# Scattering into the output itself, with a bound on the row index, and adding the head blocks four at a time

## The reference

```python
xn = _layernorm(x)
x = x + attn(xn, Wq, bq, Wk, bk, Wv, bv) + ffn(xn, g1, Wq, Wdkv, Wuk, Wuv, Wo, g2, gate_w, w1, w2)
# attn: per token, the 16 heads of that token attend to each other (16 x 16 scores of 16 values)
# ffn:  h = xn + mla(rmsnorm(xn, g1))        causal attention along the sequence, 16 heads of 16
#       h + moe(rmsnorm(h, g2))              8 experts 256 -> 512 (silu) -> 256, the two best of each token,
#                                            weighted by a softmax over their two logits
```

## Time and profile before

| | us |
|---|---|
| median of 3 runs | 2903.67 (2902.66 to 2905.32) |
| profiled execution, its own time | 2890.86 |
| its span in the trace | 2889.0 |
| PE, DVE, POOL, ACT busy | 2543.6, 2236.6, 2113.7, 1606.6 |

### The profile page before, as it was taken

How to read it: one execution, slowest core, us unless ns; L and a number is a source line. 1 busy time by engine, 2 the same in 40 slices (tenths; PEclk the granted TensorE clock), 3 DMA queues, 4 the chain that set the end, 5 groups by cost and what they waited for, 6 DMA issues and landing times. The chain is left out here.

```text
span 2889.0 us, 58374 instructions
## 1 busy us (share of the span) xinstructions
PE 2543.6 (88%) x21356; PEld 1302.9 (45%) x21356; DVE 2236.6 (77%) x3720; ACT 1606.6 (56%) x2421; POOL 2113.7 (73%) x1196
## 2 busy tenths in 40 slices
PE   7999878999999999999999999996673988988892
PEld 4544432333333333333333333224563877777782
DVE  5557858899889988998899989902563899889970
ACT  2322225677777777777777777684442544444441
POOL 4543339698889888988898889884675777778772
PEclk9999999999999999999999999997775999999996
DMA  5785552133233323332333232105865565566555
GB/s 179 228 251 196 170 183 60 49 80 93 53 85 87 93 53 85 87 93 53 84 87 93 54 85 77 44 19 161 263 213 172 116 126 124 122 127 131 126 91 145
DMA packets 235945, 334.91 MB, mean 116 GB/s; under 512 B 30024, under 2 KB 175272, under 8 KB 234920
## 3 DMA queue, kind: packets, MB, share of 16 engines
q1 hardware_dynamic: 208072, 287.54, 34.4%
q0 software_dynamic: 27360, 39.73, 8.0%
q10 hardware_dynamic: 256, 4.19, 0.4%
HBM read 246.96 MB, written 154.04 MB: 139 GB/s over the span
## 5 line engine op out<-in xcount | busy, mean ns | idle before, releaser
L1047 DVE TENSOR_REDUCE p_piece_max<-p_ring 128x1 f32<-128x512 f32 (+3 forms) x2160 | 1293.2, 654 | 136.8 <-PE p_ring L157 66.8
L1105 ACT ACTIVATE p_probs<-p_st 128x1024 f32<-128x1024 f32 (+3 forms) x1280 | 1078.8, 897 | 413.9 <-PE p_st L1168 215.7
L1168 PE MATMUL p_st<-unit_q,unit_k 64*128 64x512 bf16 (+3 forms) x3520 | 432.7, 348 | 39.5 <-ACT p_probs L1105 23.2
L1186 PE MATMUL p_pv<-p_probs,unit_vg 128*32 128x512 f32 (+3 forms) x3520 | 412.1, 543 | 0.0
L1855 POOL DMA_INDIRECT acc<-p_y,p_rows x142 | 223.3, 1573 | 142.7 <-issue 56.1
L170 PE MATMUL p_ring<-unit_k,unit_q 64*128 64x512 bf16 (+3 forms) x1600 | 271.4, 352 | 27.9 <-DVE p_piece_max L1047 25.4
L964 POOL TENSOR_TENSOR p_terms<-p_head_in 128x4096 f32<-128x4096 f32 x32 | 282.9, 8839 | 8.9 <-DMA p_head_in<-head_qkv 4.6
L985 POOL TENSOR_TENSOR p_terms<-p_head_p,p_head_in 128x4096 f32<-128x4096 f32 x32 | 283.3, 8853 | 3.6 <-ACT p_head_p L1112 3.6
L2020 PE MATMUL p_y_ps<-p_w,p_hid 128*128 128x256 f32 x1136 | 276.8, 400 | 0.0
L969 POOL TENSOR_TENSOR p_terms<-p_terms 128x2048 f32<-128x2048 f32 (+2 forms) x96 | 252.7, 2632 | 17.4 <-POOL p_terms L969 11.4
L991 POOL TENSOR_TENSOR p_terms<-p_terms 128x2048 f32<-128x2048 f32 (+2 forms) x96 | 252.6, 2631 | 17.1 <-POOL p_terms L991 11.4
(11 more groups left out here) (192 smaller groups left out, 3477.5 us busy)
## 6 DMA issues: line engine op xcount, KB each, us to landing
p_w<-ffn_w SPq DMA_DIRECT2D x142, 512.0 KB
qk_parts<-p_parts SPq DMA_DIRECT2D x64, 384.0 KB, 3.6
head_qkv<-p_heads SPq DMA_DIRECT2D x16, 1536.0 KB, 6.8
p_rows<-rows_by_expert SPq DMA_DIRECT2D x71, 258.0 KB, 3.5
unit_q<-qk_parts SPq DMA_DIRECT2D x132, 128.0 KB, 3.2
unit_k<-qk_parts SPq DMA_DIRECT2D x132, 128.0 KB, 3.6
v_padded<-p_vx SPq DMA_DIRECT2D x16, 1024.0 KB, 8.0
p_head_in<-head_qkv SPq DMA_DIRECT2D x32, 384.0 KB, 4.2
```

What stands on the lines that cost most here:

```text
L1047: nc.vector.tensor_reduce(piece_max[:, n % 2, h:h + heads, i, pc], ring_ps[g % RING][:, 0:heads * width].rearrange("p (h k) -> p h k", h=h ...
L1105: nc.scalar.activation(probs[:, 2 * turn_of(s, i) + u, :, 0:width], st_ps[u][:, :, 0:width], ACT.Exp).then_inc(probs_done, 1)
L1168: last = nc.tensor.matmul(st_ps[u][:, half, 0:width], k6[s][rows, PAIR * second + u, kt * P:(kt + 1) * P], q6[s][rows, PAIR * second + u, ...
L1186: last = nc.tensor.matmul(pv_ps[hh * VW:(hh + 1) * VW, skip:CT], vg[s][:, kt, hh * VW:(hh + 1) * VW], probs[:, 2 * turn_of(s, i) + hh % PA ...
```

## The change

`acc` is gone as a tensor of its own. Phase 3's `store_res` writes to the output, and phase 4's scatters and additions go to the output's rows. So the two phases need the output's address, and are called from `phase5_combine`; `phase3_route` and `phase4_experts` only keep their arguments until then. The order of the work on the engines is the same. The zeros behind row T are not written any more, and a token number above T - 1 in a scatter is left out by a bound on the index. The copy of `acc` to the output is left out, with its block. The head blocks' additions are made once in 8 tiles (n = 14, 22, ... 70), with four blocks (512 KB) in one DMA, 8 of them.

```diff
-def phase3_route(nc, apart, x_v, xn_v, o_v, w, sorted_rows, res_v, pos_v, gates_v, table):
+def phase3_route(*args):
+    SHARED["route"] = args
+def phase4_experts(*args):
+    SHARED["experts"] = args
+def route(nc, apart, x_v, xn_v, o_v, w, sorted_rows, res_v, pos_v, gates_v, table, out_v):
...
-    acc = SHARED["acc"] = nc.dram_tensor("acc", [T + ROW_TILE, D], F32, kind="Internal").ap()
-    acc_v = acc[0:T, :].rearrange("(b c t p) d -> b c p t d", b=B, c=NC, p=P)
...
-                sp.dma_start(acc_v[b, c], res[:, c % 2, :, :]).then_inc(res_stored[c % 2], 16)
+                sp.dma_start(out_v[b, c], res[:, c % 2, :, :]).then_inc(res_stored[c % 2], 16)
...
-            sp.dma_start(acc[T:, :].rearrange("(r p) d -> p r d", p=P), blank[:, :, 0:D]).then_inc(tail_stored, 16)
...
-            wait_apart(sp, tail_stored, 16 * 2 * E, apart)
+            wait_apart(sp, tail_stored, 16 * (2 * E - 1), apart)
...
-def phase4_experts(nc, apart, head_qkv, w, sorted_rows, expert_rows, attn_rows, table):
+def experts(nc, apart, head_qkv, w, sorted_rows, expert_rows, attn_rows, table, out_v):
...
-    sorted_rows, acc, table_i = SHARED["sorted"], SHARED["acc"], SHARED["table"]
+    sorted_rows, table_i = SHARED["sorted"], SHARED["table"]
+    acc = out_v.rearrange("b c p t d -> (b c t p) d")
...
-    ADDED = {STARTS[2 * k + 4] + 2: k for k in range(NB // 2)}
+    ADDED = {STARTS[4 * k + 6] + 2: k for k in range(NB // 4)}
...
-                if pairs[0]:
-                    pool.wait_ge(pair_added, 16 * pairs[0])
+                if fours[0]:
+                    pool.wait_ge(four_added, 16 * fours[0])
                 for t in range(RT):
                     nc.gpsimd.indirect_dma_start(
                         acc, bass.IndirectOffsetOnAxis(rows[:, n % RB, t, D + 1:].bitcast(U32), 0), y[:, n % RB, t, :], None,
-                        compute_op=ALU.add).then_inc(y_added, 16)
+                        bounds_check=T - 1, oob_is_err=False, compute_op=ALU.add).then_inc(y_added, 16)
-            def add_pair(k, tiles):
+            def add_four(k, tiles):
                 for u in range(2):
-                    pool.wait_ge(oh_stored[u], 16 * (k + 1))
+                    pool.wait_ge(oh_stored[u], 16 * 2 * (k + 1))
                 pool.wait_ge(y_added, 16 * RT * tiles)
-                n = block_of(2 * k, 1)
-                rows_of_pair = lambda a: a.rearrange("(r s) d -> r (s d)", s=8)
-                nc.gpsimd.dma_start(rows_of_pair(acc[n * P:(n + 2) * P, :]),
-                                    rows_of_pair(attn_rows[n:n + 2, :, :].rearrange("a p d -> (a p) d")),
-                                    accum_op=ALU.add, max_dma_last_dim=4 * 8 * D).then_inc(pair_added, 16)
-                pairs[0] += 1
+                n = block_of(4 * k, 0)
+                halves = lambda a: a.rearrange("(c h r s) d -> c h r (s d)", c=2, h=2, s=8)[:, 1, :, :]
+                nc.gpsimd.dma_start(halves(acc[n * P:(n + 8) * P, :]),
+                                    halves(attn_rows[n:n + 8, :, :].rearrange("a p d -> (a p) d")),
+                                    accum_op=ALU.add, max_dma_last_dim=4 * 8 * D).then_inc(four_added, 16)
+                fours[0] += 1
...
 def phase5_combine(nc, apart, res_v, attn_v, pos_v, gates_v, expert_rows, out_v):
-    acc = SHARED["acc"][0:T, :].rearrange("(b c t p) d -> b c t p d", b=B, c=NC, p=P)
-    with SHARED["stack"], ExitStack() as ctx:
-        stored = [ctx.enter_context(nc.semaphore(f"p5_stored{i}")) for i in range(2)]
-        block = ctx.enter_context(nc.Block())
-        def store(eng, i):
-            for b in range(B):
-                for c in range(i * NC // 2, (i + 1) * NC // 2):
-                    eng.dma_start(out_v[b, c].rearrange("p t d -> t p d"), acc[b, c]).then_inc(stored[i], 16)
-            wait_apart(eng, stored[i], 16 * B * NC // 2, apart)
...
+    route(*SHARED["route"], out_v)
+    experts(*SHARED["experts"], out_v)
+    SHARED["stack"].close()
```

More of the change, by code:

```diff
@@ L1734, in phase4_experts @@
     SHIFTED = {STARTS[m + 1]: m for m in range(NB)}
-    assert all(ADDED[n] * 2 + 1 in [m for at, m in STORED.items() if at < n] for n in ADDED)
-    assert max(ADDED) < N_TILE and max(STORED) < N_TILE and len(ADDED) == NB // 2 and len(LOADED) == NB - QB
+    assert all(ADDED[n] * 4 + 3 in [m for at, m in STORED.items() if at < n] for n in ADDED)
+    assert max(ADDED) < N_TILE and max(STORED) < N_TILE and len(ADDED) == NB // 4 and len(LOADED) == NB - QB
     with ExitStack() as ctx:
@@ L1788, in phase4_experts @@
         oh_stored = [sem(f"p4_oh_stored{i}") for i in range(2)]
-        pair_added = sem("p4_pair_added")
+        four_added = sem("p4_four_added")
         block = ctx.enter_context(nc.Block())
@@ L1844, in weigh @@
                     ins.then_inc(pv_done, 1)
-            pairs = [0]
+            fours = [0]
             def add_tile(n):
@@ L1880, in _ @@
                     weigh(m, slice(heads.start, heads.stop - 2), False)
-                add_pair(ADDED[n], n)
+                add_four(ADDED[n], n)
                 if weighed:
@@ L1885, in _ @@
             pool.wait_ge(y_added, 16 * RT * N_TILE)
-            pool.wait_ge(pair_added, 16 * NB // 2)
+            pool.wait_ge(four_added, 16 * NB // 4)
         @block.vector
```

## The result

The change makes the kernel slower: 2989.22 us median (2986.72 to 2990.06, 4 runs) against 2903.91 (4 runs), ratio 1.0292, interval 1.0274 to 1.031. Forecast were 2859 us, and 2885 at most.

A forecast was written before the change was run, and what follows sets the result against it. POOL with its pair additions was taken to bound the expert stage, DVE close behind. Terms of -32.9, -12.9, -0.8 and +2.0 summed to -44.6 us, taking 2903.67 to 2859 us; range 2837 to 2885.

The forecast's parts named there:

- Part 2: Four-block additions in place of pairs in the expert stage: 2.4 us more landing, 66.15 us per 8-tile cycle against 70.7.
- the check: The bound on the row index in each of the 142 scatters, forecast to cost 0.15 us a scatter.
- part 4: Stage edges: -0.8 us where the pair at n = 66 goes, +2.0 us behind the stage.
- Closing copy: End of the kernel: dropping the copy to the output saves 32.9 us, or 29.7 if the block's closing stays.
- Part 3: Index bound on the scatters: 0.15 us each, +2.4 us per 8-tile cycle, making it 68.55 us.
- rival A: The scatters' index check is free, b near 0: 15.0 us less, 2844 us; chance 0.22.
- Rivals C and D: Dear scatter check: C 0.30 to 0.45 us, 2874 to 2889 us, chance 0.17; D 0.58 us, 2908 us, chance 0.07.
- Blank tile: Tile 70's last scatter moves nothing, so part of its landing goes: -1.2 us.
- Edges: Around the stage: n = 10 pair's removal 0; last addition +2.6 us on the final path; +2.0 us behind the stage.
- Phase 3: Stores go to the output instead of the internal tensor: 0, at best -0.5 us.
- Rival B: The four-block addition lands almost as fast as the pair, +0.6 us: 12.6 us less, 2846 us; chance 0.14.
- landing 7.1 us: Sign to look for in the profile: the four-block addition's DMA lands in 7.1 us, its duration near 1.1.

The follow-up runs named there:

- f1_spread: The changed kernel, its four-block 512 KB DMA reordered so 32 pieces of 8 KB are outermost and the two halves inside: 2845.31 us, ratio 0.982.
- f2_two_dmas: The changed kernel, with the four blocks added by two 256 KB DMAs one behind the other, once in 8 tiles: 2839.5 us, ratio 0.9805.
- b1_bound: The kernel before, with only the bound on the rows of the adding scatters added: 2897.05 us, ratio 0.9994.
- f3_pairs: The changed kernel, with pairs added every 4 tiles as before; output as target, bound, missing zeros and missing copy stay: 2866.32 us, ratio 0.9891.
- b0_same: The kernel before, unchanged, profiled a second time: 2895.07 us, span 2893.2.

## Why the prediction was wrong

Part 2 is the step that failed. It took "2 x 1.2 = 2.4 us more of landing" from the pair's two bursts, and bounded it by 4.7, "all of the landing again"; measured were 18.5 (23.2 less 4.7). What I did not ask is how the new shape would be dealt out over the engines. Both bounds assumed that it would be dealt out like the old one. With 18.5 in place of 2.4 and no price for the check, the part's own sum gives 49.35 + 14.2 + 18.5 + 0.2 = 82.3 us a cycle; measured are 510.7 / 6 = 85.1. The other 2.8 us are not assigned: PE waits 90.3 us for rows between n = 14 and n = 62, against 47.1 before, so the ring of four tiles runs dry more, but f1_spread, where PE waits only 36.9, lies 2.0 us over the same sum as well (67.7 against 49.35 + 14.2 + 2.0 + 0.2 = 65.75).

The bursts themselves were read wrongly too, and that 2.4 fits a spread DMA is in part luck. A digit of the earlier trace rows counts the whole time of the packets that start in its slice, so the zeros between the bursts are no pause. The 16 packets that start between 2846.5 and 2847.2 in the kernel before have a share of 174.9% of 16 engines in that 0.7 us, which is 1.22 us each, and the second burst starts as they end; the 16 between 2847.7 and 2848.3 have 104.8% of 0.6 us, 0.63 us each. So 1.2 us is the price of the first piece on an engine, and a further one costs 0.6. In f1_spread's last addition the bursts start 7, 4 and 3 slices of 0.175 us apart, and it lands in 5.3 us where the last pair took 4.1: two more pieces cost 1.2 us there. Its median, 6.7 us, is 2.0 above the pair's 4.7, near the 2.4 forecast; the difference, when other engines work and other DMAs run, no experiment explains.

The frame in which this term stood holds in its total. POOL is the bound and all of the landing is exposed. Without the check's price and with the closing's other end (-29.7), the prediction's own sum gives 2859 - 15.0 + 3.2 = 2847 us, a ratio of 0.981; f1_spread, the change as it was meant, has 0.982. But two misses cancel in it. Cycles of 8 tiles were to gain 6 x 4.55 = 27.3 us without the check and gain 18.1 in f1_spread (67.7 us a cycle against 66.15 forecast; f2_two_dmas, from 2362.59 at n = 14 to 2764.28 at n = 62, has 66.95), while the stretch from n = 62 to 70 gains 7.6 us where part 4 had 0.8 (56.8 us against 64.3; the other profiles with pairs have 60.6 to 63.5 there). Why that stretch gains so much was not looked into.

- **Closing copy**, -32.9 with 29.7 as the other end: the other end is right. The span ends 3.7 us behind the last scatter's last packet, where I took 0.4; that is about the 3.6 us which the closing of phase 4's block took before, and I read it as the same closing, though no run isolates it. Between b1_bound and f3_pairs, 0.9994 and 0.9891, lie the copy with its block, and the output as target: together 1.0% of the time, 30 us.
- **Part 3, the bound**, b = 0.15 us a scatter: it is nothing that can be measured, rival A's case: b1_bound's interval ends at 1.0003, which is 0.9 us, and at 10 us for each 0.1 that leaves b 0.01 at most. Rivals C and D, the dear check, had 0.24 of the chances between them. The kernel did become slower, but by another way than D's.
- **Blank tile**, -1.2: the scatter moves nothing, as forecast.
- **Edges**: the last addition costs 19.0 us more on the final path, for the same reason as in part 2. The first pair's leaving gave 4.0 us in the table where I took 0; over all profiles, phase 4's start to n = 14 takes 128.1 to 130.0 us with that pair and 125.9 to 127.3 without it, which is some 2.5 us.
- **Phase 3**, 0: right as far as the eight other profiles show. The 16.6 us of the table are 11 of spread and 5.6 that no run assigns. I moved the sum from a profiled execution 12.8 us below the median. That it was an odd one in phase 3 does not explain the gap: b0_same begins phase 4 10.9 us later, but its span is only 4.2 us longer (2893.2), because it needs 655.8 us from there to the end where the first profile needs 662.6.

Rival B asked how the landing grows with bytes, and expected 0.6 us for the second 256 KB; with the pieces spread it is 1.2 us for the last addition and 2.0 to 2.2 by the medians (f1_spread's 6.7 against 4.7, or f3_pairs' 4.5), above that rival.

There is a rule that decides this, and I did not weigh it. The Trainium skill, DMA: Bandwidth & Descriptors, section "Why a DMA increments its semaphore by 16 and not by 1", says that the number of engines is the largest one up to 16 that divides the slowest dimension not of size 1 on both sides of the DMA, and that software can split a contiguous run so that it goes over all. The traces agree in three shapes: outermost 2, two engines' rate (28 GB/s); outermost 4, twice that (54 GB/s); outermost 32 (f1_spread) or one contiguous run (the pairs), bursts of all. By that rule, as an estimate, the change's DMA has 32 pieces in a row on each engine where the pair has 2. The price of the 30 more pieces comes from the trace of the kernel before, at the 0.63 us of the pair's second pieces: 19 us, against 18.5 measured. It could have been had before the run, and with it the direction: some 16 us more than forecast in each of 6 cycles outweigh the 44.6 us of the sum.

The prediction's list of signs was of use: the scatters stayed at 1.57 us, which spoke against the check at once, and "landing 7.1 us" against 23.2 named the culprit in one row.

## What to carry to other kernels

When a DMA's shape changes, count its pieces per DMA engine before its bytes: read the outermost dimension as the hardware gets it. Here 2 and 4 there meant two and four engines' rate, and 32 meant all. A gap in what was one contiguous run was enough to take this DMA from 16 engines to 2. Two ways out were measured, and both worked: the small dimension put inside (f1_spread), and one DMA per run (f2_two_dmas). Where a wait is wholly exposed, as the landing is here, its upper bound has to include the case that the transfer runs on few engines. And when a row of DMA activity shows bursts, ask how long a packet takes before calling the space between them a pause.

## What the runs showed of the hardware that was not expected

- While two engines carried the data, the DMA still made 464 small packets, 448 of 8 bytes and 16 of 4; with an outermost dimension of 4 it made 400. The counts fit 32 small packets on each engine without data (14 x 32 and 12 x 32) and one more on each of the 16; the trace does not name a packet's engine.
- A DMA of 1 MB over four engines lands in 24.0 us, one of 512 KB over two in 23.2: the time follows the pieces in a row. For an addition between DRAM and DRAM, a piece of 8 KB takes 0.63 us, and 1.0 to 1.7 us when it is the first on its engine.
- A bound on the row index of an adding scatter costs nothing in the instruction (1566 against 1567 ns) or in the time (ratio 0.9994). A scatter of 128 rows above the bound moves no data, but still makes 128 packets of 8 bytes and 16 of 4 (288 packets for two scatters).
